# Rotated queries turned by VectorE and carried over a DRAM buffer, their low part made by GpSimd; five queues reordered, scores masked in place

## The chip, the cores and the metric

One core of a Trainium2 chip runs the whole kernel: TensorE (PE), VectorE (DVE), ScalarE (ACT), GpSimd (POOL) and the SyncE queue (SP), which issues most transfers. The metric is the device time of one execution in microseconds (us). All instruction streams are in order; they meet at semaphores written out by hand.

## The reference

Eight sequences of 128 tokens and width 512 go through four residual layers. The change touches only the first, attention over a paged cache:

```
q, k, v = x Wq, x Wk, x Wv          # 32 query heads, 8 key heads, D = 128
q, k = rope(rmsnorm(q)), rope(rmsnorm(k))
keys, values = 16 cached pages of 32 rows (512) + the 128 new ones
scores = q keys^T / sqrt(D), cached keys beyond the length masked
x = x + softmax(scores) values Wo
```

The others are a dense layer with a sign mask, a SwiGLU layer with LoRA, and an adapter product.

## The kernel before, in words

Every fp32 product is made of three passes over a high and a low part (`three_pass`, L65 to L67): ScalarE writes the high part (`hi`, L682), VectorE or GpSimd subtracts it from the source to get the low part (`lo`, L932; GpSimd L541, L546, L550, L555, L561).

Attention loops over 8 groups g (a key head with its 4 query heads) and in each over the 8 sequences b. One (g, b) is called a step here. Groups 1 to 6 are one hardware loop on every engine, group 0 and group 7 are written out. A step works on three sequences at once: it multiplies the probabilities of (g, b) with the values, makes the scores of the next one (g1, b1), and projects the one after that (g2, b2). Each engine has its own `group` function, which lists its work of a step in order. In the order before TensorE does: nine 128x128 transposes of probabilities (heads 0 to 2, chunks 0 to 2), four of the rotated queries of (g1, b1) (`queries`, L1227), three more of probabilities (head 3), the output product of the preceding sequence, the transpose of the new keys (L1221), the query projection of (g2, b2), scores 0 and 1, values 0 and 1, scores 2 and 3, values 2, the key and value projection, values 3 and 4.

Scores leave PSUM by one VectorE instruction that adds the mask, scales, and takes the maximum (`mask_and_max`, L984) into one of two buffers `scores`; ScalarE takes the exponential into `probs` (`exps`, L730), VectorE inverts the sum (`inverse`, L990), GpSimd scales (`normalise`, L565). Chunks 3 and 4 of the probabilities are not transposed by TensorE: VectorE turns their 32x32 squares (`turn_squares`, L1011), SP writes them to the DRAM buffer `turned_rows` (512 KB, L382) and reads them back as four transfers of 128 KB with the squares in their places (L385). ScalarE and VectorE then split them as they do the others (`probs_T`).

Queries: TensorE projects, VectorE multiplies with cosines and sines (`turn_q`, L961 and L963), GpSimd adds (`rotate_q`, L509 and L510), TensorE transposes into bank 4 (L1227), ScalarE copies the high part and VectorE makes the low one (`queries`), and score 0 waits for it on `qT_done`.

In steps b = 1 to 4 of groups 1 to 6 GpSimd also gathers a quarter of the next group's pages into `kv_stage` (`stage_pages`, L497, 1 MB each; in b = 1 and 3 it first computes new page numbers, L492 and L494), and SP stores it in the DRAM buffers `kT_pages` or `v_pages` (L377). Step b = 4 loads the next group's Wq and Wkv (L333, L334), step b = 5 splits them; step b = 0 splits Wo. SP loads keys and values of (g2, b2) in every step (L359, L365). ScalarE splits these values one step later, in (g1, b1)'s place (`cached_values`).

## Time and profile before

| | us |
|---|---|
| median of 3 runs | 1328.85 (1328.2 to 1328.89) |
| profiled execution: its own time / its span | 1327.64 / 1325.9 |
| PE busy | 1302.4 (98%) |
| DVE busy | 1037.4 (78%) |
| ACT / POOL busy | 843.8 / 844.0 (64%) |

The span is what the profile covers, the execution's own time is 1.74 us more. Engines overlap, so the busy times do not add up.

### The profile page before, as it was taken

What the parts mean: (1) busy time and instruction counts of PE and PEld (TensorE: products, weight loads), DVE (VectorE), ACT (ScalarE), POOL (GpSimd) and SP (SyncE); (2) the same over time, 40 slices, a digit from 0 to 9 for tenths busy, and PEclk for the clock granted to TensorE, in tenths of its full rate; (3) what the DMA queues carried; (4) which work ended last, traced back from release to release, by engine and by line L of the source; (5) the groups of instructions that cost most, each with busy time, mean ns of one, the idle gap of its engine ahead of it and who ended that gap; (6) DMA issues with size and microseconds to landing.
All of it is one profiled execution on the core that took longest, in us unless ns stands there. A gap on an engine that the chain in (4) does not pass through costs nothing.

```text
span 1325.9 us, 25249 instructions
## 1 busy us (share of the span) xinstructions
PE 1302.4 (98%) x7316; PEld 1135.4 (86%) x7316; DVE 1037.4 (78%) x2235; ACT 843.8 (64%) x2217; POOL 844.0 (64%) x1116
## 2 busy tenths in 40 slices
PE   9898999999999999999999999999999899999999
PEld 8787888888888888888888888888888688888887
DVE  7977887888787878787888788778888886748546
ACT  7566666766676656666766676666666774635444
POOL 7677777777777767777777786777766832415111
PEclk9999999999999999999999999999999999999999
DMA  5578658745874687468547844884554453454542
GB/s 204 193 212 270 151 143 230 243 127 158 228 215 130 177 238 196 130 183 259 143 127 221 270 110 127 231 274 107 190 132 114 133 171 129 138 177 154 181 140 80
DMA packets 215388, 233.14 MB, mean 176 GB/s; under 512 B 134817, under 2 KB 174369, under 8 KB 204577
## 3 DMA queue, kind: packets, MB, share of 16 engines
q1 hardware_dynamic: 209568, 196.24, 51.0%
q0 software_dynamic: 5760, 36.18, 8.6%
q8 instruction: 29, 0.48, 0.2%
q14 instruction: 31, 0.25, 0.1%
...
## 4 chain that ended last, share of the span: by engine, by line
PE 88%; DVE 8%; POOL 2%; issue 1%; ACT 1%; DMA 1%; SPq 0%; DVEq 0%; POOLq 0%; ACTq 0%
PE ps L65 26%; PE ps L66 25%; PE ps L67 25%; PE ps L1245 5%; DVE at_scores L984 2%; DVE at_pT_lo L932 2%; PE ps L1227 2%; DVE shared L1452 1%; PE ps L2196 1%; PE ps L1287 1%; DMA at_pT_raw<-turned_rows 1%; PE ps L1221 0%; DVE at_turned L1011 0%; POOL at_probs L565 0%; PE ps L2229 0%
## 5 line engine op out<-in xcount | busy, mean ns | idle before, releaser
L730 ACT ACTIVATE at_probs<-at_scores,at_neg_max 128x640 f32<-128x640 f32 x256 | 211.4, 826 | 250.7 <-DVE at_neg_max L984 250.3
L565 POOL TENSOR_SCALAR at_probs<-at_probs,at_row_inv 128x640 f32<-128x640 f32 x256 | 223.1, 876 | 129.7 <-DVE at_row_inv L990 128.5
L984 DVE CUSTOM_DVE_ANT_0 at_scores<-ps,at_mask,at_inv_rms 128x640 f32<-128x640 f32 x256 | 220.3, 879 | 30.8 <-PE ps L67 29.0
L65 PE MATMUL ps<-ds_hi,x_hi 128*128 128x512 f32 (+1 forms) x564 | 198.5, 352 | 0.8 <-DVE x_lo L1502 0.4
L67 PE MATMUL ps<-ds_hi,x_lo 128*128 128x512 f32 (+1 forms) x564 | 192.5, 341 | 0.0
L65 PE MATMUL ps<-at_kT_hi,ds_lo 128*128 128x320 f32 x512 | 159.2, 311 | 9.4 <-DVE at_neg_max L984 6.7
L67 PE MATMUL ps<-at_kT_hi,ds_lo 128*128 128x320 f32 x512 | 158.8, 310 | 0.0
L66 PE MATMUL ps<-at_kT_lo,ds_lo 128*128 128x320 f32 x512 | 158.7, 310 | 0.0
L932 DVE TENSOR_TENSOR at_pT_lo<-ps,at_pT_hi 128x512 fp32r<-128x512 f32 x196 | 133.8, 684 | 7.0
L65 PE MATMUL ps<-at_pT_hi,at_v_hi 128*128 128x512 f32 x320 | 129.6, 405 | 6.6 <-DVE at_pT_lo L932 6.1
L66 PE MATMUL ps<-at_pT_lo,at_v_hi 128*128 128x512 f32 x320 | 126.5, 395 | 0.0
L67 PE MATMUL ps<-at_pT_hi,at_v_lo 128*128 128x512 f32 x320 | 125.3, 391 | 0.0
L65 PEld LDWEIGHTS ps<-ds_hi,x_hi 128*128 128x128 f32 x564 | 106.7, 189 | 19.9 <-DVE x_lo L1502 0.8
L66 PE MATMUL ps<-ds_lo,x_hi 128*128 128x512 f32 x308 | 120.2, 390 | 0.0
L67 PEld LDWEIGHTS ps<-ds_hi,x_lo 128*128 128x128 f32 x564 | 105.9, 188 | 13.1
L509 POOL TENSOR_TENSOR at_q_rot<-ds_bias,a_raw 128x256 f32<-128x256 f32 x64 | 47.5, 741 | 105.7 <-DVE a_raw L963 105.7
L1011 DVE STREAM_TRANSPOSE at_turned<-at_probs 128x256 f32<-128x256 f32 x248 | 97.7, 425 | 18.4 <-POOL at_probs L565 18.4
L65 PEld LDWEIGHTS ps<-at_kT_hi,ds_lo 128*128 128x128 f32 x512 | 96.7, 189 | 17.5 <-DVE at_neg_max L984 8.7
L65 PE MATMUL ps<-at_woT_hi,at_oT_hi 128*128 128x512 f32 x256 | 107.1, 418 | 1.3 <-DVE at_oT_lo L932 1.3
L1245 PE MATMUL ps<-ident,at_probs 128*128 128x128 f32 x784 | 106.4, 272 | 0.0
L682 ACT ACTIVATE at_pT_hi<-ps 128x512 fp32r<-128x512 f32 x196 | 102.5, 600 | 4.3 <-PE ps L67 4.0
L67 PE MATMUL ps<-at_woT_hi,at_oT_lo 128*128 128x512 f32 x256 | 100.7, 394 | 0.0
...
## 6 DMA issues: line engine op xcount, KB each, us to landing
...
kv_raw<-kT_pages SPq DMA_DIRECT2D x60, 256.0 KB, 5.4
...
kv_raw<-v_pages SPq DMA_DIRECT2D x56, 256.0 KB, 4.7
...
```

Of the source, the lines that this page charges most:

```text
L65: pe.matmul(out, l_hi, r_hi, start=first, stop=False)
L66: pe.matmul(out, l_hi, r_lo, start=False, stop=False)
L67: return pe.matmul(out, l_lo, r_hi, start=False, stop=last)
L509: pool.tensor_tensor(q_rot[:, :, 0:HALF], u_q[:, :, 0:HALF], w_q[:, :, HALF:D], ALU.subtract)
L565: pool.tensor_scalar(probs[:, h, :], probs[:, h, :], row_inv[:, h:h + 1], 1.0, ALU.mult, ALU.mult).then_inc(probs_done, 1)
L682: act.activation(out, src, ACT.Copy).then_inc(done, 1)
L730: act.activation(probs[:, h, :], scores[h % 2][:], ACT.Exp, bias=neg_max[:, h:h + 1], scale=-1.0, accum_out=row_sum[:, h:h + 1]).then_inc( ...
L932: dve.tensor_tensor(out, src, hi_part.bitcast(F32), ALU.subtract).then_inc(done, 1)
L984: dve.tensor_tensor_reduce(out=scores[h % 2][:], in0=slot(h), in1=mask[:, b, :], scale=inv_rms[b % 2][:, h:h + 1], scalar=3.0e38, op0=ALU. ...
L1011: dve.transpose(turned[:, :, :, h, :].rearrange("p k c r -> p c k r"), probs[:, h, (KC - MOVED) * P:KEYS].rearrange("p (c k i) -> p c k i" ...
L1227: ins = pe.transpose(bank(Q_BANK)[:, h * S:(h + 1) * S], q_rot[:, h, :], ident[:])
L1245: return pe.transpose(bank(probs_bank(b, c))[:, h * S:(h + 1) * S], probs[:, h, c * P:(c + 1) * P], ident[:])
```

## The change

The rotated queries of all steps but the first two of group 0 no longer go through TensorE. VectorE turns their 32x32 squares in one instruction of 128x512 (`spread_queries`); SP writes them with four transfers into a new DRAM buffer `q_rows` (`store_queries`, 256 KB) and in the next step, right behind the write of `turned_rows`, reads them back with one (`read_queries`, 256 KB). ScalarE makes the high part from there, GpSimd the low part (`queries` of pool).

The orders of all five queues change with it. TensorE projects before it makes the output product, which comes right ahead of score 0, and waits for `y_added` ahead of values 0; score 2 stands between values 0 and 1. VectorE takes its wait for GpSimd's `rotate_q` (in `spread_queries`) ahead of `mask_and_max` 2; the low part of chunk 3 stands ahead of `mask_and_max` 3; heads 0 and 1 share one reciprocal, heads 0 to 2 one turn of squares; the new values' low part moves to the end of the step before, ahead of the last head's squares. GpSimd makes `key_scale` first, then the gather, `cached_keys`, `rotate_k`, `queries`, `cached_values`, the weights' parts, `rotate_q` and the four `normalise`. ScalarE splits cached and new values of (g2, b2) at the end of the step, one step earlier than before, and takes the squares of the queries ahead of the exponentials. One of the two Wq parts that GpSimd made in step b = 6 goes to VectorE in b = 5, the other to GpSimd in b = 5; VectorE's two both stand in b = 5. The masked scores are written into `probs`, and the exponential works there in place. In group 0 GpSimd makes five of the cosine tables in place of four. Four semaphores are merged with others and two added, and single loads of indices are moved in SP's queue of the last group. Of the diff, cut to its core (SP, GpSimd, ScalarE, VectorE, TensorE in this order):

```diff
...
-        scores = [sb(f"scores{j}", [P, KEYS]) for j in range(2)]
...
+        q_turned_rows = sb("q_turned_rows", [P, NQ, G, SQ])
+        qT_raw = sb("qT_raw", [P, NQ, G, SQ])
...
+        def q_by_moves(g, b):
+            return not (isinstance(g, int) and g == 0 and b < 2)
+        def q_moves(g, b, k):
+            return upto(g, b, (NQ + 1) * 16) - 2 * (NQ + 1) * 16 + k * 16
...
+                if not (isinstance(g, int) and (g, b) == (HK - 1, B - 1)) and q_by_moves(*following(g, b)):
+                    read_queries(*following(g, b))
...
+            def store_queries(g, b):
+                wait_apart(sp, q_spread, upto(g, b, 1, 1) - 2, passed)
+                for a in range(NQ):
+                    sp.dma_start(q_rows.rearrange("(k i) (a n) -> a i k n", k=NQ, a=NQ)[a],
+                                 q_turned_rows[a * SQ:(a + 1) * SQ].rearrange("i k h r -> i k (h r)")).then_inc(q_moved, 16)
+            def read_queries(g, b):
+                wait_apart(sp, q_moved, q_moves(g, b, NQ), passed)
+                sp.dma_start(qT_raw[:].rearrange("p a h r -> p (a h r)"), q_rows).then_inc(q_moved, 16)
...
+                    if not (last and b >= B - 2):
+                        store_queries(g2, b2)
...
+            def queries(g, b):
+                wait_apart(pool, qT_hi_done, upto(g, b, 1, 1), passed)
+                l, h = (t[b % 2].rearrange("p (h a r) -> p h a r", h=G, a=NQ) for t in (qT_lo, qT_hi))
+                pool.tensor_tensor(l, qT_raw[:].rearrange("p a h r -> p h a r"), h.bitcast(F32), ALU.subtract).then_inc(qT_done, 1)
...
+                    key_scale(g2, b2)
...
-                    if b == B - 2 and not last:
-                        wq_group(g + 1, 2)
+                    if started and not keys_by_row(g1, b1):
                         cached_keys(g1, b1)
-                        wq_group(g + 1, 3)
-                    key_scale(g2, b2)
-                    if started and not keys_by_row(g1, b1) and b != B - 2:
-                        cached_keys(g1, b1)
+                    rotate_k(g2, b2)
                     if started:
+                        queries(g1, b1)
                         cached_values(g1, b1)
                     if b == B - 3 and not last:
                         qkv_group(g + 1, DC)
...
                     if b == 0:
                         wo_group(g, 0)
                         wo_group(g, 1)
...
                     rotate_q(g2, b2)
-                    normalise(g1, b1, 0)
-                    rotate_k(g2, b2)
-                    for h in range(1, G):
+                    for h in range(G):
                         normalise(g1, b1, h)
...
+                    if b == B - 3 and not last:
+                        wq_group(g + 1, 3)
...
+                if upto(0, b, 1) >= 2 or not (isinstance(g, int) and g == 0):
+                    act.wait_ge(pv_done, upto(g, b, KC) - KC - 1)
...
+                if upto(0, b, 1) >= 2 or not (isinstance(g, int) and g == 0):
+                    act.wait_ge(pv_done, upto(g, b, KC) - KC)
...
-                act.activation(probs[:, h, :], scores[h % 2][:], ACT.Exp, bias=neg_max[:, h:h + 1], scale=-1.0,
+                act.activation(probs[:, h, :], probs[:, h, :], ACT.Exp, bias=neg_max[:, h:h + 1], scale=-1.0,
...
+                if q_by_moves(g, b):
+                    hi(qT_hi[b % 2].rearrange("p (h a r) -> p h a r", h=G, a=NQ), qT_raw[:].rearrange("p a h r -> p h a r"),
+                       q_moved, q_moves(g, b, NQ + 1), qT_hi_done)
...
                         attended(*preceding(g, b))
+                    else:
+                        queries(g1, b1)
+                    probs_T(g, b, 0)
+                    probs_T(g, b, 1)
+                    new_keys(g1, b1)
+                    if started:
                         cached_keys(g1, b1)
-                        new_values(g1, b1)
-                    queries(g1, b1)
+                    probs_T(g, b, 2)
+                    if b == B - 3 and not last:
+                        qkv_group(g + 1, DC)
                     if started:
-                        cached_values(g1, b1)
-                    for c in range(KC - MOVED):
-                        probs_T(g, b, c)
-                    new_keys(g1, b1)
+                        queries(g1, b1)
+                    if b == B - 3 and not last:
+                        qkv_group(g + 1, DC + 1)
...
                             probs_T(g, b, c)
+                    squares(g2, b2)
...
-                        for n in (DC, DC + 1, *range(DC)):
+                        for n in range(DC):
                             qkv_group(g + 1, n)
                     exps(g1, b1, 0)
                     exps(g1, b1, 1)
...
                             probs_T(g, b, c)
                     exps(g1, b1, 2)
                     exps(g1, b1, 3)
-                    squares(g2, b2)
                     if not (last and b == B - 3):
                         key_squares(*following(g2, b2))
+                    cached_values(g2, b2)
+                    new_values(g2, b2)
...
-                dve.tensor_tensor_reduce(out=scores[h % 2][:], in0=slot(h), in1=mask[:, b, :],
+                dve.tensor_tensor_reduce(out=probs[:, h, :], in0=slot(h), in1=mask[:, b, :],
...
+            def two_inverses(g, b):
+                dve.wait_ge(exp_done, upto(g, b, G, 2))
+                dve.reciprocal(row_inv[:, 0:2], row_sum[:, 0:2]).then_inc(inv_done, 2)
...
+            def turn_first_heads(g, b, n):
+                dve.wait_ge(probs_done, upto(g, b, G, n))
+                dve.transpose(turned[:, :, :, 0:n, :].rearrange("p k c h r -> p h c k r"),
+                              probs[:, 0:n, (KC - MOVED) * P:KEYS].rearrange("p h (c k i) -> p h c k i", c=MOVED, k=NQ)).then_inc(turned_done, n)
+            def spread_queries(g, b):
+                dve.wait_ge(q_rot_done, upto(g, b, 1, 1))
+                dve.transpose(q_turned_rows[:].rearrange("p k h r -> p h k r"),
+                              q_rot[:].rearrange("p h (k i) -> p h k i", k=NQ)).then_inc(q_spread, 1)
...
                         attended(*preceding(g, b))
+                    else:
+                        queries(g1, b1)
+                    probs_T(g, b, 0)
                     if b == 1:
                         wo_group(g, 3)
-                    if b == B - 2 and not last:
-                        qkv_group(g + 1, 1)
-                    queries(g1, b1)
+                    probs_T(g, b, 1)
                     if started and keys_by_row(g1, b1):
                         cached_keys(g1, b1)
+                    new_keys(g1, b1)
...
+                        probs_T(g, b, 2)
...
                     if started:
-                        new_values(g1, b1)
-                    probs_T(g, b, 0)
...
+                        turn_k(g2, b2)
+                    turn_q(g2, b2, 0)
+                    turn_q(g2, b2, 1)
                     if started:
-                        add_y(*preceding(g, b), last and b > 0)
-                    probs_T(g, b, 1)
-                    new_keys(g1, b1)
-                    probs_T(g, b, 2)
...
-                        turn_q(g2, b2, 0)
-                        turn_q(g2, b2, 1)
+                        probs_T(g, b, 2)
...
                             probs_T(g, b, c)
...
+                        turn_k(g2, b2)
                     if started:
-                        turn_q(g2, b2, 0)
-                        turn_q(g2, b2, 1)
+                        add_y(*preceding(g, b), last and b > 0)
                     mask_and_max(g1, b1, 0)
                     mask_and_max(g1, b1, 1)
-                    turn_k(g2, b2)
+                    spread_queries(g2, b2)
...
                     if b == 0:
                         wo_group(g, 2)
...
-                    inverse(g1, b1, 0)
                     if b == B - 3 and not last:
                         qkv_group(g + 1, 0)
                     mask_and_max(g1, b1, 2)
-                    inverse(g1, b1, 1)
-                    mask_and_max(g1, b1, 3)
+                    two_inverses(g1, b1)
                     if by_moves(g, b):
                         probs_T(g, b, 3)
...
+                    if b == B - 3 and not last:
+                        qkv_group(g + 1, 1)
+                    mask_and_max(g1, b1, 3)
                     inverse(g1, b1, 2)
                     if by_moves(g, b):
                         probs_T(g, b, 4)
...
+                    if b == B - 3 and not last:
+                        qkv_group(g + 1, 2)
                     inverse(g1, b1, 3)
-                    if by_moves(g1, b1):
-                        for h in range(G):
-                            turn_squares(g1, b1, h)
+                    turn_first_heads(g1, b1, G - 1)
...
+                    new_values(g2, b2)
+                    turn_squares(g1, b1, G - 1)
...
-                    pe.wait_ge(qT_done, upto(g, b, 1))
+                    if by_row(g) and b == 2:
+                        pe.wait_ge(qT_done, 2)
+                    else:
+                        pe.wait_ge(q_squared, upto(g, b, 1))
...
-                    queries(g1, b1)
...
+                        queries(g1, b1)
                     probs_T_rest(g, b)
-                    if started:
-                        output(*preceding(g, b))
                     new_keys(g1, b1)
...
                             probs_T(g, b, c)
                     project_q(g2, b2, range(DC))
+                    if started:
+                        output(*preceding(g, b))
...
                         times_v(g, b, 0)
                         times_v(g, b, 1)
...
                     pe.wait_ge(pT_done, upto(g, b, KC, KC - MOVED if by_moves(g, b) else KC))
                     score(g1, b1, 1)
                     if by_moves(g, b):
+                        pe.wait_ge(*((dense.x1_ready, b) if last and b else (y_added, upto(g, b, 1))))
                         times_v(g, b, 0)
+                    score(g1, b1, 2)
+                    if by_moves(g, b):
                         times_v(g, b, 1)
-                    score(g1, b1, 2)
                     score(g1, b1, 3)
...
```

## Rows read from the trace of the kernel before

**Rows 1.** The page's busy time of each engine, and the chain that ended last.

```profile
PE 1302.4 (98%) x7316; PEld 1135.4 (86%) x7316; DVE 1037.4 (78%) x2235; ACT 843.8 (64%) x2217; POOL 844.0 (64%) x1116
...
PE 88%; DVE 8%; POOL 2%; issue 1%; ACT 1%; DMA 1%; SPq 0%; DVEq 0%; POOLq 0%; ACTq 0%
```

**Rows 2.** By stretch, steps b = 0, 1, 4, 5 of group 1: PE, PEld, DVE, ACT, POOL busy, clock, DMA.

```profile
172.00:188.30 16.30, 16.21 (x97) 14.20 (x95) 13.50 (x32) 12.26 (x34) 12.35 (x17) 1.00 0.38 98
188.30:204.20 15.90, 15.90 (x95) 14.04 (x94) 13.11 (x32) 9.79 (x30) 11.71 (x18) 1.00 0.83 232
...
235.90:251.70 15.80, 15.80 (x94) 13.99 (x93) 12.48 (x31) 10.08 (x30) 11.00 (x16) 1.00 0.97 295
251.70:267.50 15.80, 15.80 (x95) 14.03 (x94) 13.07 (x32) 13.17 (x36) 12.66 (x17) 1.00 0.48 141
```

**Rows 3.** The chain of waits from 616 us (start, length).

```profile
616.62 0.98 PE ps L1245 x9
617.61 0.44 PE ps L1227 x4
618.04 0.33 PE ps L1245 x3
```

**Rows 4.** Transfers, stretches 602.4:604.1 and 636.9:640: packets, MB, share of 16 engines.

```profile
q1 hardware_dynamic: 144, 0.52, 76.4%
...
q1 hardware_dynamic: 528, 0.49, 54.0%
```

**Rows 5.** GpSimd's groups of instructions, 160 to 940 us.

```profile
L565 POOL TENSOR_SCALAR at_probs<-at_probs,at_row_inv 128x640 f32<-128x640 f32 x196 | 170.0, 873 | 97.2 <-DVE at_row_inv L990 97.0
L561 POOL TENSOR_TENSOR at_v_lo<-kv_raw,at_v_hi 128x512 fp32r<-128x512 f32 x50 | 64.4, 1289 | 0.0
...
L509 POOL TENSOR_TENSOR at_q_rot<-ds_bias,a_raw 128x256 f32<-128x256 f32 x49 | 36.1, 738 | 80.2 <-DVE a_raw L963 80.2
```

**Rows 6.** VectorE's timeline in a step b = 5.

```profile
643.30 0.67 DVE L932 TENSOR_TENSOR ds_lo<-staging,ds_hi 128x512 fp32r<-128x512 f32 x1
644.07 0.88 DVE L984 CUSTOM_DVE_ANT_0 at_scores<-ps,at_mask,at_inv_rms 128x640 f32<-128x640 f32 x1
...
645.75 0.82 DVE L932 TENSOR_TENSOR at_pT_lo<-at_pT_raw,at_pT_hi 128x512 fp32r<-128x512 f32 x1
...
647.24 1.15 DVE L1011 STREAM_TRANSPOSE at_turned<-at_probs 128x256 f32<-128x256 f32 x3
```

**Rows 7.** ScalarE's timeline, 603 to 606 us.

```profile
603.28 1.56 ACT L682 ACTIVATE at_pT_hi<-ps 128x512 fp32r<-128x512 f32 x3
605.49 0.28 ACT L682 ACTIVATE at_kT_hi<-ps 128x128 fp32r<-128x128 f32 x1 [0.64 <-PE ps L1221]
```

**Rows 8.** SP's timeline, steps b = 3 and 4.

```profile
601.79 0.33 SPq L382 DMA_DIRECT2D turned_rows<-at_turned  x1
604.48 1.75 SPq L385 DMA_DIRECT2D at_pT_raw<-turned_rows  x4
...
624.99 5.55 SPq L365 DMA_DIRECT2D kv_raw<-v_pages  x1
```

**Rows 9.** GpSimd's timeline: a page number and gather (b = 3), the Wkv parts (b = 5).

```profile
602.48 0.25 POOL L492 TENSOR_SCALAR at_page_row<-at_page_row 128x1 f32<-128x1 f32 x1
...
603.98 1.10 POOL L497 DMA_INDIRECT shared<-in_kT_cache,at_page_idx  x1 [0.89 <-POOL at_page_idx L494]
605.11 0.20 POOL L516 TENSOR_TENSOR at_inv_rms<-at_sumsq,at_d_eps 128x1 f32<-128x1 f32 x1
...
638.14 2.57 POOL L546 TENSOR_TENSOR ds_hi<-at_wkv_raw,ds_hi 128x512 fp32r<-128x512 f32 x2 [0.68 <-ACT ds_hi L682]
```

**Rows 10.** Transfers by issue in b = 4, then b = 5; the last number is us to landing.

```profile
kv_raw<-v_pages SPq DMA_DIRECT2D x1, 256.0 KB, 8.2
...
kv_raw<-v_pages SPq DMA_DIRECT2D x1, 256.0 KB, 4.1
```

**Rows 11.** By stretch, columns as in Rows 2: step b = 3 of group 0.

```profile
85.60:104.30 18.70, 16.57 (x94) 13.90 (x93) 12.96 (x32) 10.18 (x31) 13.38 (x19) 1.00 0.81 211
```

**Rows 12.** By stretch, columns as in Rows 2: a step of group 7.

```profile
983.70:1000.00 16.30, 16.02 (x95) 14.05 (x93) 14.14 (x33) 10.02 (x30) 9.98 (x15) 1.00 0.43 99
```

129 lines of the change are left out of this document (64 added, 65 removed).

## The prediction

> **What bounds the kernel now.** I read the page's first and fourth parts first: TensorE is busy 98% of the span and makes 88% of the chain that ended last [rows 1]. Then the busy time by stretch, step by step: in groups 1 to 6 a step takes 15.8 us and TensorE is busy in all of it, whether the transfer engines are at 0.48 or at 0.97 of their time; only b = 0 takes 16.3 [rows 2]. So in 48 steps every TensorE instruction counts in full, and the other engines have about 3 us of cover each. The chain of waits shows where the removed instructions lie. What the change does to the cover must be read from the orders of the queues.
>
> **What is taken off.** Four transposes, 0.44 us, stand in the chain [rows 3]. 62 steps lose them (64 less the first two): 27.3 us, 0.44 in each, which makes a step of 15.4 us if all else stays hidden. No other TensorE work is added.
>
> **What is added.** On the transfer engines: the write of `turned_rows` moved 0.52 MB in 76.4% of 1.7 us, 1.3 us, and the reads of 1 KB packets 0.49 MB in 54% of 3.1 us, 1.7 us [rows 4]. 256 KB therefore cost 0.65 to 0.85 us; `q_rows` is written and read in each step, and its writes go in packets of 512 B, so 1.7 us a step, 0.11 of a step. On GpSimd: `queries`, 128x512 of two inputs, as L561, 1.29 us [rows 5]. On VectorE: three turns of 128x256 take 1.15 us, so 128x512 takes 0.8, against 0.67 for the low part that leaves [rows 6]. VectorE's sum is unchanged; its order is not.
>
> The Trainium skill ("VectorE: DVE Perf Modes", Rules for kernel authors) says that a 128x128 transpose belongs on TensorE where PSUM will do. By it the 0.44 us on TensorE are the cheap form; the rows say cheap for the other engines only, since TensorE is the one that has no room.
>
> **A plain step, walked.** t counts from the first of the nine transposes. 0.98 + 0.33 [rows 3] end at 1.3; new keys, projection and output (24 matmuls of 0.23 us) end at 7.0, where score 0 is due; the last two value products start at 14.1 and 14.8, and t = 15.4 is the next step. ScalarE gets head 3 at about 1.7, takes two chunks at 0.52, new keys 0.28, cached keys 0.6 [rows 7]: 3.7. GpSimd then makes cached keys 1.25, `rotate_k` 0.6, `queries` 1.25 [rows 5]: 6.8. Score 0 waits for that: 0.2 us of margin. The read of `q_rows` starts behind the turned write, which is issued at about 1.2 and lands 2.7 later [rows 8]; with 0.8 for its own data it lands at 4.7, ScalarE is done at 5.3, GpSimd is free at 5.5. So b = 7 gains its 0.44 in full. GpSimd then makes cached values (8.1) and `rotate_q`, two of 0.74 [rows 5], 9.6; VectorE turns the queries behind `mask_and_max` 1 by 10.4, ahead of score 2: hidden too.
>
> **b = 5 and b = 0.** GpSimd has two weight parts ahead of `rotate_q`, 2.57 us [rows 9]. In b = 5: 8.1 + 2.6 = 10.7, `rotate_q` 12.1, the turn of queries 12.9. VectorE waits in it, and all the rest of its list is queued behind: a Wq part 0.6 (13.5), mask 2 0.8 (14.3), chunk 3 0.8 (15.1), a Wq part 0.6 (15.7), mask 3 0.8 (16.5), chunk 4 0.65 (17.2) [rows 6]. Values 4 are due at 14.8: 2.4 us late, and the normalised heads after it too. Before, only GpSimd's own scaling waited for `rotate_q`. In b = 0 one part less stands there, and none between chunk 3 and mask 3: 16.6 against 14.8, 1.8 us. These two need no assumption on transfers; below, they are 1.2 and 2.0.
>
> **b = 1 to 4.** The gather is issued ahead of `cached_keys`. In b = 1 and 3 it costs GpSimd 2.6 us with its page number (602.48 to 605.11), in b = 2 and 4 1.1 [rows 9]. Head 3's scaling ends at about 0, the two scales add 2.15, 2.6 make 4.8, and 1.25 + 0.6 + 1.25 end at 7.9: score 0 is 0.9 late. A late head 3 adds to it; 0.6 to 1.9, I take 1.0. In b = 2 and 4 GpSimd is in time, but the gather's 1 MB starts while the read of `q_rows` is under way. Alone it lands at 4.7; if it shares the engines to the gather's end it lands up to 1.6 us too late. I take half, 0.8.
>
> The Trainium skill ("DMA: Bandwidth & Descriptors", Queues, rings and completion order) has each transfer engine take turns between queues packet by packet. By that the read would end with the gather, 1.6 us late in both steps, and the sum would be 10 us higher; no row here shows this read beside a gather.
>
> **The values, one step early.** ScalarE's `cached_values` now stands at the end of the step in which its load is issued. In b = 5 that load lands in 4.1 us, in b = 4, behind Wq and Wkv, 8.2 us after 624.99, at 633.2 [rows 8, 10]. The values' last product of that step would end at 616.62 + 15.4 = 632.0 [rows 3]. New values, the attended rows and head 3's squares stand behind it in ScalarE's and VectorE's queues, and TensorE's key transpose waits for the new values' low part. With the engines at 0.97 [rows 2] and 1.7 us more to move, the load comes later still: 1.5 to 3 us, of which some is covered by the late chunk 4 of the next step. I take 0.8 more in b = 5 (3.2 in all) and 0.5 left over in b = 6.
>
> **The sum.** Per group: 1.8 + 1.0 + 0.8 + 1.0 + 0.8 + 3.2 + 0.5 + 0 = 9.1 us of new waits against 8 x 0.44 = 3.5: +5.6, and 6 groups give +33. In group 0 steps take 18.7 us, with GpSimd busy 13.4 of them and transfers at 0.81 [rows 11]: it is bound by the chain through both, which gets 1.3 us of GpSimd and 1.7 of transfers longer. Over five such steps I take +5, between 0 and +10, the 0.44 counted in. In group 7 VectorE is busy 14.1 of 16.3 us [rows 12]; its sum stays, and chunk 4 comes to stand behind a piece of the dense layer's weights: -1 to +3 with the 0.44 counted in, I take 0. 1327.64 + 38 = 1365.6; the profiled execution stood 1.2 us under the median, so 1367 against a median of 1328.85.
>
> Bounds: with the lower ends (1.2, 0.6, 0, 0.6, 0, 2.0, 0, 0 = 4.4 a group) +0.9 a group, 5 in all, and -1 outside: 1333. With the upper ends (1.8, 1.9, 1.6, 1.9, 1.6, 4.5, 0.7, 0 = 14.0) +10.5 a group, 63, and +13 outside: 1405.
>
> **The rivals.**
> A, this forecast, new waits outweigh the transposes: 1333 to 1385.
> B, the other side: GpSimd and VectorE catch up, so the waits are not lost. The place is `rotate_q` ahead of the turn of queries in b = 0 and b = 5; if VectorE's late list costs TensorE under 3.5 us a group in all, the kernel is faster. For it: before, TensorE had no wait in b = 5 with GpSimd at 12.7 busy of 15.8 [rows 2]. Against: the walk gives 4.2 in these two steps alone. With nothing late it is 1328.85 - 27.3 = 1301.5, with half the lower ends 1315.
> C, transfers become the bound. b = 4 at 0.97 plus 0.11 no longer fits in its step, and what is left pushes the turned write, chunks 3 and 4, and the values of the next. For it: 0.83 in b = 1 becomes 0.94. Against: b = 0 and 5 stay under 0.6 with it. 1385 to 1405.
> D, gains and waits cancel: within 0.2% of before, which is about what a measurement of this kernel can tell from no change.
>
> A 0.55, B 0.20, C 0.20, D 0.05. So slower 0.75, same 0.05, faster 0.20. The range takes A, D, most of C and the near part of B: 1315 to 1398; A's own is 1333 to 1385.
>
> **What would show it.** L1227 down to 8 transposes. In the chain of waits of b = 0 and 5, VectorE at L984 and L932, released by GpSimd at L509; a wait of the turn of queries for GpSimd of 2 us there and none in b = 7. Score 0 late by GpSimd's `queries` in b = 1 and 3. ScalarE waiting for `v_pages` in b = 4. Steps of 15.4 us for b = 7, about 17 for b = 0, 18 for b = 5. The prediction is wrong if TensorE's idle time stays under 3.5 us a group: then GpSimd's list ran earlier than walked, or `rotate_q` was not late.

## The result and the profile after

The changed kernel takes 1426.85 us in the median of 4 runs (1424.84 to 1429.76), the kernel before 1328.53 (4 runs): a ratio of 1.0742, 95% interval 1.0723 to 1.0761. It is slower, as forecast, but by 98 us where 38 were forecast, and outside the range of 1315 to 1398. The profiled execution took 1429.76 us for a span of 1427.9, 102.0 above the span before.

The page, busy time and then the chain that ended last, answers to [rows 1]:

```profile
PE 1305.6 (91%) x7068; PEld 1108.7 (78%) x7068; DVE 1038.7 (73%) x2054; ACT 856.8 (60%) x2217; POOL 938.4 (66%) x1173
...
PE 46%; DMA 16%; DVE 11%; POOL 11%; issue 9%; SPq 3%; ACT 3%; POOLq 0%; DVEq 0%; ACTq 0%
```

TensorE was 88% of the chain and is 46%; transfers, VectorE and GpSimd share the rest. The stretch of groups 1 to 6, first before and then after, shows where it went (length, then PE, PEld, DVE, ACT, POOL busy, clock, DMA share, GB/s):

```profile
172.00:935.50 763.50, 762.94 (x4420) 673.66 (x4418) 616.97 (x1465) 510.02 (x1453) 554.97 (x757) 1.00 0.65 186
```

```profile
184.50:1031.10 846.60, 765.67 (x4225) 651.57 (x4224) 621.63 (x1327) 520.70 (x1452) 626.49 (x799) 0.99 0.72 197
```

In these 48 steps TensorE had 0.6 us of idle time before and has 80.9 after. It has 192 transposes fewer, 21 us by [rows 3], and is still busy 2.7 us longer: what is left runs longer. The three parts of the 102.0: 12.5 us in group 0 (group 1 starts at 184.5 against 172.0), 83.1 in groups 1 to 6, 6.4 behind. The steps of group 1, b = 0, 1, 4 and 5, answer to [rows 2]:

```profile
184.48:202.56 18.08, 16.34 (x92) 13.80 (x91) 13.25 (x29) 12.67 (x34) 13.82 (x18) 1.00 0.47 117
202.56:219.96 17.40, 15.68 (x90) 13.48 (x89) 12.84 (x29) 10.26 (x30) 13.37 (x19) 1.00 0.88 240
255.46:274.51 19.05, 15.91 (x90) 13.46 (x89) 12.85 (x28) 10.28 (x30) 13.75 (x19) 0.99 0.90 274
274.51:294.38 19.87, 17.89 (x83) 15.00 (x82) 14.25 (x31) 12.97 (x35) 14.07 (x14) 0.84 0.49 134
```

Here and below a step's length is the time from one issue of the turned write to the next, mean over groups 2 to 6:

```
b              0     1     2     3     4     5     6     7    sum
before       16.4  15.9  15.8  15.8  15.8  15.8  15.8  15.8  127.3
after        19.9  17.8  15.9  17.1  18.4  19.9  15.6  16.0  140.8
forecast     17.2  16.4  16.2  16.4  16.2  18.6  15.9  15.4  132.3
```

The waits of the changed kernel (engine, what it does, who releases it: us in all, times, longest):

```profile
ACT ds_lo L716 <- DMA at_qT_raw<-q_rows: 102.4, 57, 3.2
PEld ps L65 <- issue: 78.9, 59, 3.7
...
DVE at_q_turned_rows L1072 <- POOL at_q_rot L540: 32.7, 16, 3.0
...
PE ps L65 <- POOL ds_lo L590: 22.8, 11, 3.3
...
ACT at_v_hi L716 <- DMA kv_raw<-v_pages: 14.5, 6, 3.4
ACT at_oT_hi L716 <- issue: 13.5, 5, 3.0
PE ps L1284 <- DVE at_v_lo L1024: 12.8, 7, 2.9
```

The waits that the forecast named are there: ScalarE waits for the value pages six times, VectorE for `rotate_q` 16 times, TensorE for GpSimd's low part. The lengths are not: b = 7, 0 and 5 take 16.0, 19.9 and 19.9 us where 15.4, about 17 and 18 were forecast. Two rows were not in it. ScalarE waits for the queries' read in nearly every step, and five times 2.7 us for nothing visible ("issue").

### The profile page after: what moved, and what is told of

Read it like the earlier page. It is cut to its first block, busy times and chain, and to the rows that moved or that the text cites. A ratio compares the mean times of both kernels' runs of the same rounds, so it can differ in the third digit from the quotient of the medians.

```text
span 1427.9 us, 25340 instructions
## 1 busy us (share of the span) xinstructions
PE 1305.6 (91%) x7068; PEld 1108.7 (78%) x7068; DVE 1038.7 (73%) x2054; ACT 856.8 (60%) x2217; POOL 938.4 (66%) x1173
## 4 chain that ended last, share of the span: by engine, by line
PE 46%; DMA 16%; DVE 11%; POOL 11%; issue 9%; SPq 3%; ACT 3%; POOLq 0%; DVEq 0%; ACTq 0%
PE ps L65 14%; PE ps L66 13%; PE ps L67 13%; DMA at_pT_raw<-turned_rows 6%; DMA kv_raw<-v_pages 4%; DMA turned_rows<-at_turned 3%; DVE at_probs L1031 3%; POOL at_probs L600 3%; PE ps L1308 2%; DVE at_pT_lo L979 2%; DMA at_qT_raw<-q_rows 2%; SPq L401 2%; POOL at_woT_lo L580 1%; DVE at_turned L1066 1%; POOL ds_hi L576 1%
## 5 line engine op out<-in xcount | busy, mean ns | idle before, releaser
L600 POOL TENSOR_SCALAR at_probs<-at_probs,at_row_inv 128x640 f32<-128x640 f32 x256 | 250.9, 990 | 176.8 <-DVE at_row_inv L1041 150.6
L768 ACT ACTIVATE at_probs<-at_probs,at_neg_max 128x640 f32<-128x640 f32 x256 | 211.8, 828 | 223.7 <-DVE at_neg_max L1031 223.7
L1031 DVE CUSTOM_DVE_ANT_0 at_probs<-ps,at_mask,at_inv_rms 128x640 f32<-128x640 f32 x256 | 224.2, 881 | 96.6 <-PE ps L67 93.6
L979 DVE TENSOR_TENSOR at_pT_lo<-ps,at_pT_hi 128x512 fp32r<-128x512 f32 x196 | 128.8, 681 | 4.2 <-ACT at_pT_hi L716 4.2
L66 PE MATMUL ps<-at_pT_lo,at_v_hi 128*128 128x512 f32 x320 | 127.3, 398 | 0.0
L716 ACT ACTIVATE at_pT_hi<-ps 128x512 fp32r<-128x512 f32 x196 | 111.1, 602 | 26.4 <-PE ps L1308 22.1
L979 DVE TENSOR_TENSOR at_pT_lo<-at_pT_raw,at_pT_hi 128x512 fp32r<-128x512 f32 x124 | 106.4, 858 | 21.2 <-ACT at_pT_hi L716 21.1
L67 PEld LDWEIGHTS ps<-ds_hi,x_lo 128*128 128x128 f32 x564 | 106.7, 189 | 13.5
L585 POOL TENSOR_TENSOR at_kT_lo<-kv_raw,at_kT_hi 128x512 fp32r<-128x512 f32 x60 | 77.1, 1286 | 45.1 <-ACT at_kT_hi L716 44.3
L65 PEld LDWEIGHTS ps<-at_pT_hi,at_v_hi 128*128 128x128 f32 x320 | 60.6, 189 | 57.6 <-DVE at_pT_lo L979 55.4
L65 PE MATMUL ps<-at_woT_hi,at_oT_hi 128*128 128x512 f32 x256 | 100.5, 393 | 1.5 <-DVE at_oT_lo L979 1.4
L1308 PE MATMUL ps<-ident,at_probs 128*128 128x128 f32 x784 | 100.6, 277 | 1.1 <-POOL at_probs L600 0.9
```

The source lines that it names most:

```text
L65: pe.matmul(out, l_hi, r_hi, start=first, stop=False)
L66: pe.matmul(out, l_hi, r_lo, start=False, stop=False)
L67: return pe.matmul(out, l_lo, r_hi, start=False, stop=last)
L585: pool.tensor_tensor(in_pages(kT_lo[:, 0:L]), pages_keys(k_raw[b % 2]), in_pages(kT_hi[:, 0:L]).bitcast(F32), ALU.subtract).then_inc(kc_do ...
L600: pool.tensor_scalar(probs[:, h, :], probs[:, h, :], row_inv[:, h:h + 1], 1.0, ALU.mult, ALU.mult).then_inc(probs_done, 1)
L716: act.activation(out, src, ACT.Copy).then_inc(done, 1)
```

## The experiments

A ratio is against the kernel before.

**e1, e2, e3, e4: single waits, and what the transposes were worth.** In e1 `spread_queries` moves behind the fourth mask:

```diff
                     mask_and_max(g1, b1, 1)
-                    spread_queries(g2, b2)
...
                     mask_and_max(g1, b1, 3)
+                    spread_queries(g2, b2)
```

> The changed kernel with one move: VectorE's turn of the rotated queries (and with it its wait for GpSimd's rotate_q) stands behind the fourth score's mask instead of behind the second's. Theory 1 (VectorE's wait in b=0 and b=5 is on the path): the changed kernel waits 16 times for rotate_q, 32.7 us in all, 2.0 us each, with masks 2 and 3 queued behind; with the move these waits vanish and the time falls by 16 to 32 us, to 1395 to 1411. Theory 2 (the trip of the queries over DRAM is the path): the turn starts some 3 us later in six of eight steps, the read lands as much later, ScalarE's wait for it (102.4 us in all, 57 times) grows, and the time stays or rises, to 1425 to 1460. Theory 3 (GpSimd's own order, rotate_q behind the parts of wo and wkv, sets these steps whatever waits on VectorE): within 5 us of 1427.

It took 1498.69 us (1.1271, 1.1251 to 1.1291), 72 us more than the change: theory 2, the trip over DRAM is on the path, and by more than was thought. ScalarE's wait for the read rose:

```profile
ACT ds_lo L716 <- DMA at_qT_raw<-q_rows: 173.8, 62, 5.0
```

Not all of the 72 us is waiting: TensorE's busy time rose from 1305.6 to 1339.0 us at a mean granted clock of 0.962 against 0.993.

e2 issues the read ahead of SyncE's wait for the turned probabilities:

```diff
                     if by_moves(g, b):
+                        if q_by_moves(*following(g, b)):
+                            wait_apart(sp, qT_done, upto(g, b, 1, 1), passed)
+                            read_queries(*following(g, b))
                         move_turned(g, b)
```

> The changed kernel with one move on the DMA issuing queue: the read of the turned queries is issued ahead of SyncE's wait for the turned probabilities (once the raw buffer's last reader is through), not behind it and behind the write. Theory 1 (ScalarE's wait for that read, 1.8 us in nearly every step, holds squares and the exps behind it and so the path): the wait falls below 0.5 us and the time falls by 60 us or more, to under 1370. Theory 2 (the wait is idle time that ScalarE has over, since the exps behind it wait for scores anyway): the wait vanishes and the time falls by under 10 us, 1417 to 1427. Theory 3 (the DMA engines are the bound in the tail of the step): the read now delays other transfers, above all the gather's, and the time is within 5 us or slower.

It took 1406.64 (1.0576, 1.0557 to 1.0595), 20 us less than the change, between theories 1 and 2. The wait fell from 102.4 us to this:

```profile
ACT ds_lo L717 <- DMA at_qT_raw<-q_rows: 11.5, 11, 4.6
```

Of 91 us of ScalarE's waiting 20 were on the path. The step b = 7 fell from 16.0 to 15.3 us: the plain step of the forecast, 15.4, is there once the read is in time. b = 5 fell by 1.3 us too, and b = 0 rose from 19.9 to 20.7.

e3 puts ScalarE's and VectorE's halves of the values back into the following step:

```diff
-                    cached_values(g2, b2)
-                    new_values(g2, b2)
...
                     if started:
+                        new_values(g1, b1)
                         attended(*preceding(g, b))
...
                         queries(g1, b1)
+                        cached_values(g1, b1)
```

> The changed kernel with ScalarE's and VectorE's halves of the values put back into the following step, where the kernel before had them (new values ahead of the attended values, cached values behind the queries). Theory 1 (in b=4 ScalarE waits 2.1 us for the value pages and with it everything behind, 14.5 us over six groups; TensorE waits 12.8 us more, seven times, for the new values behind): both waits vanish, b=4 is shorter by 2 to 3 us, and the time falls by 15 to 25 us, to 1402 to 1412. Theory 2 (the halves cost the same wherever they stand, and in the following step they lie ahead of the probabilities' eviction, on the path): the six steps without a wait grow by about 1 us each and the time rises by 20 to 50 us.

It took 1424.8 (1.0713, 1.0694 to 1.0732), 2 us less. b = 4 fell from 18.4 to 16.6 us, as theory 1 said, but b = 0 and b = 5 rose from 19.9 to 21.5 and 21.1, as theory 2 did. The value pages' wait was real, and taking it away by this move was worth nothing.

e4 leaves three of four query transposes out of the kernel before, from (0, 2) on, so heads 1 to 3 score with old queries:

```diff
-                for h in range(G):
+                for h in range(1 if upto(0, b, 1) >= 2 or not (isinstance(g, int) and g == 0) else G):
                     ins = pe.transpose(bank(Q_BANK)[:, h * S:(h + 1) * S], q_rot[:, h, :], ident[:])
```

> The kernel before with one of the four query transposes on TensorE in each step from the second group's start on (heads 1 to 3 of the bank then hold old queries): what the three transposes' TensorE time, 0.33 us by the row of the chain, is worth by itself, with nothing else moved. Theory 1 (TensorE's stream sets every step, the prediction's term of 0.44 us for four): the time falls by 0.33 x 62 = 20 us, to 1308. Theory 2 (the steps are set by the evictions on VectorE and ScalarE, which stay): it falls by under 7 us, 1322 to 1329.

It took 1329.52 (0.9996, 0.9986 to 1.0006): theory 1 fell. Three quarters of the saving that the forecast credited at 0.44 us a step are worth nothing in the old order. The chain of waits of e4 over a step shows why (lines of TensorE left out between 460.51 and 471.32):

```profile
459.87 0.60 DVE at_oT_lo L932
460.47 0.04 issue
460.51 0.50 PE ps L65
...
471.58 0.80 DVE at_scores L984
472.38 0.01 DVE at_neg_max L984
472.39 0.74 DVE at_pT_lo L932
...
474.44 0.81 POOL at_probs L565
475.26 0.02 issue
475.28 0.45 DVE at_turned L1011
475.73 0.59 DVE at_oT_lo L932
```

From the attended values' low part (459.87) through TensorE's output product, projection and scores to the fourth mask, its normalisation, its turn and the next attended low part (475.73) it is 15.86 us, and the transposes are not in it. The kernel before had two loops of one length, TensorE's own and this one. TensorE at 98% busy showed only the first.

**e5, e8, e9: trip or reordering?** e5 is the changed order with the queries turned on TensorE again:

```diff
                     probs_T_part(g, b)
-                    if not started:
-                        queries(g1, b1)
+                    queries(g1, b1)
                     probs_T_rest(g, b)
...
-                    spread_queries(g2, b2)
...
-                        store_queries(g2, b2)
```

> The changed kernel with the rotated queries turned on TensorE again (transposes ahead of the last head's probabilities, high part by ScalarE and low part by VectorE out of the bank, right behind the attended values, as the kernel before had them); no VectorE spread, no store, no read, no low part on GpSimd. All other reorderings of the change stay. Theory 1 (the trip of the queries over DRAM costs the time): 1330 to 1350, within 2% of the kernel before. Theory 2 (the reordered queues cost it, GpSimd's four normalisations in one burst and the output behind the projection above all): 1395 to 1430. Halves: near 1375.

It took 1416.27 (1.0644, 1.0625 to 1.0663). That looked like theory 2, the reordering costs it all. But the kernel has a wait that neither parent has:

```profile
PE ps L65 <- DVE ds_lo L949: 71.6, 61, 2.9
```

The projection waits for the queries' low part in the bank that it writes. In the kernel before, the output product stood between them. So e5 doesn't price the reordering by itself.

e8 is the kernel before with the scores in place and the five DMAs of the queries added, unused; e9 has the scores in place alone:

```diff
+                    if not (last and b >= B - 2):
+                        store_queries(g2, b2)          # e8: out of q_rot, read into a tile that nobody uses
...
-                dve.tensor_tensor_reduce(out=scores[h % 2][:], in0=slot(h), in1=mask[:, b, :],
+                dve.tensor_tensor_reduce(out=probs[:, h, :], in0=slot(h), in1=mask[:, b, :],
```

> The kernel before with the scores masked in place and, added, the store of the rotated queries (four DMAs) and the read (one) at the same places of SyncE's queue as in the change; the queries still go over TensorE, what is read is used by nobody. It prices the traffic and the issuing alone. Theory 1 (the traffic and the waits in SyncE's queue are hidden, only the dependence of the scores on the trip costs): within 5 us of the kernel before, 1325 to 1335. Theory 2 (the DMA engines or SyncE's queue are near their bound in the tail of the step, so the read of the turned probabilities and the loads behind land later): 1350 to 1400.

> The kernel before with one edit: the scores are masked into the probabilities' tile and the exp works in place there; the two score tiles are gone. No engine gets more work. Both theories of the change take it as free: 1326 to 1331. Should the mask of a head have to wait for that head's probabilities of the step before, it would cost 0.5 us or more a step, over 1360.

e9 took 1330.01 (1.0002, 0.9993 to 1.0012): free. e8 took 1341.37 (1.0089, 1.0072 to 1.0105): traffic and issuing cost 12 us, and 6.9 of them lie in group 0 (group 1 starts at 178.9 against 172.0). In groups 2 to 6 the eight steps add up to 127.7 us against 127.3, with b = 4 longer by 1.1 and b = 5 shorter by 0.9. (In e8 GpSimd's `rotate_q` also waits for an earlier store, so the 12 us are an upper price for traffic and issuing.) Nobody waits for the read here. So the load on the transfer engines isn't the cause by itself; what waiting for the landing costs, e8 doesn't tell.

**e7, e6: moves together, and the wait for `rotate_q` alone.** e7 joins e2 and e3 and moves `rotate_q` ahead of GpSimd's weight parts; e6 does the last alone:

```diff
                         cached_values(g1, b1)
+                    rotate_q(g2, b2)
                     if b == B - 3 and not last:
                         qkv_group(g + 1, DC)
...
-                    rotate_q(g2, b2)
```

> The changed kernel with three moves together: the read issued ahead of SyncE's wait for the turned probabilities (alone it gave 1406.6), ScalarE's and VectorE's halves of the values back in the following step (alone 1424.8), and GpSimd's rotate_q in b=0 and b=5 ahead of the parts of wo and wkv. If the waits that each removes are separate: 20 us, 2 us and, for 16 waits of 2 us, 15 to 30 us, so 1375 to 1390. If the steps with these waits are set by something behind them all (the turned probabilities' trip, or GpSimd's burst): 1400 to 1407, the read alone.

> The changed kernel with GpSimd's rotate_q ahead of the parts of wo (b=0) and of wkv (b=5), where VectorE waits 2.0 us for it. The prediction charged 3.2 us a group to b=5 and 1.8 to b=0 for this. If it was right, the time falls by up to 30 us, to 1397; if the weights' parts only come later and hold up what waits for them, or another wait lies right behind, it falls by under 8 us.

e6 took 1406.85 (1.0587, 1.057 to 1.0605), 20 us less: b = 0 from 19.9 to 18.2 us and b = 5 from 19.9 to 18.4. The forecast's place was right. e7 took 1395.92 (1.0504, 1.0479 to 1.0529), 31 us less where the three parts give 42.

**e10: ScalarE's jump back.** The five waits for "issue" lie at the start of groups 2 to 6. ScalarE's timeline there:

```profile
606.34 0.28 ACT L757 ACTIVATE at_v_hi<-ps 128x128 fp32r<-128x128 f32 x1
609.22 0.60 ACT L716 ACTIVATE at_oT_hi<-ps 128x512 fp32r<-128x512 f32 x1 [2.60 <-issue]
```

```diff
-            with act.Fori(1, HK - 1) as g:
+            for g in range(1, HK - 1):
                 group(g, False)
```

> The changed kernel with ScalarE's loop over groups 1 to 6 written out as straight code; the other engines keep their loops, and every engine has the same operations in the same order. In the changed kernel ScalarE waits 2.4 to 3.0 us for nothing that the profile shows ahead of the attended values in b=0, in just the five groups that begin with a jump back (13.5 us in all), and the steps of b=0 last 19.9 us where the kernel before had 16.3. Theory 1 (the jump back makes ScalarE wait for its instructions, and the change has put an operation that waits for TensorE last in the loop, so that no queued work covers the jump): the five waits vanish and the time falls by 10 to 15 us, to 1412 to 1417. Theory 2 (the wait is for something else at the group's start, say for what the weights' parts of the new group need): no change, within 4 us of 1427.

It took 1415.98 (1.0651, 1.0618 to 1.0683), 11 us less; the five waits are gone and b = 0 fell to 18.1 us. The page's row of the queue that brings instructions (packets, MB, share) tells what they were; first before, then after, then e10:

```profile
q14 instruction: 31, 0.25, 0.1%
```

```profile
q14 instruction: 56, 0.46, 0.1%
```

```profile
q14 instruction: 41, 0.34, 0.1%
```

The changed kernel moves 25 packets of instructions more, and the waits stand right behind a jump back. The kernel before has no such wait: there ScalarE stood idle for 0.25 us ahead of the same operation, for TensorE:

```profile
552.77 0.60 ACT L682 ACTIVATE at_oT_hi<-ps 128x512 fp32r<-128x512 f32 x1 [0.25 <-PE ps L67]
```

The Trainium skill ("Runtime: NRT & Kernel Launch", Instruction fetch mechanics) says that a taken branch whose target isn't among the two pages that an engine holds must fetch it by DMA before it goes on; the traces agree (waits of 2.5 to 3.0 us and 56 packets with the jump, no wait and 41 packets without). No run measured the size at which ScalarE's loop stops fitting.

**e11, e12, e13: single orders put back.** e11 is e5 with the output product ahead of the projection; e12 and e13 are the change with one VectorE order undone:

```diff
                     probs_T_rest(g, b)
+                    if started:
+                        output(*preceding(g, b))       # e11
...
+                    inverse(g1, b1, 0)                 # e12
                     mask_and_max(g1, b1, 2)
-                    two_inverses(g1, b1)
+                    inverse(g1, b1, 1)
...
                     mask_and_max(g1, b1, 3)
+                    if by_moves(g, b):                 # e13, ahead of the mask in the change
+                        probs_T(g, b, 3)
```

> The kernel with the queries turned on TensorE and the changed orders (it took 1416.3) with one more thing put back: TensorE's output product of the attended values stands ahead of the projection of the queries, as in the kernel before. There the projection waited 1.15 us in nearly every step (71.6 us in all, 61 times) for VectorE's low part of the queries, in the bank that it writes to. Theory 1 (that wait is all that the plain steps of that kernel lose): plain steps fall from 16.9 to about 15.9 and the time to 1350 to 1365; what is left over the kernel before is the price of the other reorderings. Theory 2 (output's own inputs, the attended values' low part, are as late as the queries' low part): 1400 to 1416.

> The changed kernel with the inverses of heads 0 and 1 made apart again, head 0's ahead of the third mask and head 1's behind it, so that GpSimd can start its four normalisations earlier. Theory 1 (in many steps the burst of four, 3.81 us, ends 1 us behind the last inverse and so delays the turn and with it the whole trip of the probabilities): plain steps get shorter by 0.5 to 1 us and the time falls by 20 to 50 us. Theory 2 (the last normalisation waits for the last inverse anyway): within 6 us, and the added instruction on VectorE, 0.15 us a step, may cost up to 9.

> The changed kernel with VectorE's low part of the first moved chunk of the probabilities behind the fourth mask again, as in the kernel before; it is ahead of it in the change, so that a late landing of the turned probabilities holds up the fourth mask, its exp, its normalisation and the next turn, the loop from trip to trip. Theory 1 (that loop sets b=1, b=3 and b=4, where ScalarE is seen to wait for the landing): each of these shorter by 0.5 to 1 us, 10 to 18 us in all, 1409 to 1417. Theory 2 (the landing also holds ScalarE's exps, so the loop goes on through them): within 5 us of 1427.

e12 took 1419.8 (1.0674, 1.065 to 1.0698), 7 us less, just over theory 2's bound; the plain steps b = 6 and 7 stayed at 15.6 and 16.1. e13 took 1435.37 (1.0794, 1.0771 to 1.0818), 8 us more: both theories fell. e11 took 1455.5 (1.0954, 1.0923 to 1.0984), 39 more than e5. Its waits:

```profile
ACT at_kT_hi L693 <- PE ps L1244: 138.5, 61, 4.1
...
PEld ps L65 <- DVE at_pT_lo L949: 106.1, 85, 2.0
```

The output product put the new keys' transpose later, and the change has ScalarE wait for those keys ahead of the cached keys and the third chunk. One order put back into a set that was made for another only makes a new wait.

**e15, e14: the trip in the old order, and the best of the new.** e15 is the kernel before with the trip and nothing else of the reordering (and the scores in place). e14 is the change with e3, e6, e10 and e12, and e2's read in all steps but b = 0.

```diff
                     inverse(g1, b1, 0)
+                    spread_queries(g2, b2)             # e15, VectorE
...
                     for c in range(KC - MOVED):
                         probs_T(g, b, c)
+                    if started:
+                        queries(g1, b1)                # e15, ScalarE, out of qT_raw
```

> The kernel before with the trip of the queries alone, and every queue else in its old order: VectorE spreads the rotated queries ahead of the third mask, SyncE stores and reads them as in the change, ScalarE takes the high part behind the first probabilities' evictions, GpSimd the low part ahead of its low part of the cached values, TensorE turns none. Scores masked in place. Theory 1 (the trip costs what its transfers cost, 12 us, and its late landing some 20 more at most; the rest of the 98 us is the reordering): 1335 to 1365. Theory 2 (the trip is the cost, and the reordering is what it takes to bear it): 1400 or more.

> The changed kernel with what helped, together: the read ahead of the wait for the turned probabilities in all steps but b=0, the halves of the values in the following step, rotate_q ahead of the parts of wo and wkv, the inverses of heads 0 and 1 apart, ScalarE's loop written out. Three of these together took 1395.9; the inverses gave 7 us and the loop 11 us alone. If these are separate costs: 1375 to 1382. If one hides another: 1385 to 1396. Either way it stays over the kernel before, unless the steps of b=0 to b=5 fall to 16 us, which no part so far did.

e15 took 1428.46 (1.0739, 1.0721 to 1.0757): theory 1 fell clearly. The trip put into the old order costs just what the whole change costs. Its plain steps b = 2 and b = 7 are 15.8 us, as before: without the transposes, and nothing gained. Its b = 0 and b = 5 take 22.4 and 20.0 us. ScalarE in b = 0, and its wait in all:

```profile
601.40 0.23 ACT L752 ACTIVATION_READ_ACCUMULATOR at_square<-ps 128x1 f32 x1
606.00 0.60 ACT L718 ACTIVATE at_oT_hi<-ps 128x512 fp32r<-128x512 f32 x1 [4.37 <-issue]
```

```profile
ACT ds_lo L718 <- DMA at_qT_raw<-q_rows: 109.3, 57, 5.1
```

The jump back costs it 22.6 us in five waits of ScalarE, the longest 5.1. Like e5, e15 has a wait of its own making: its high part of the queries stands in ScalarE's queue ahead of the new keys' (in the change, behind them), so what ScalarE waits for the read holds up the keys too. So its 99 us are the price of the trip at this place of the queue. No run has it at another place in the old order. e14 took 1369.89 (1.0303, 1.0286 to 1.032), 57 us less than the change and better than its expectation; it is the best version of the change that ran, and slower than the kernel before. Its plain steps are 15.0 and 15.3 us; b = 1 to 5 take 16.3 to 18.2.

**e16, e17: ScalarE's squares.** e16 is the kernel before with one call moved; e17 moves it in the changed kernel:

```diff
+                    squares(g2, b2)                    # e16, ahead of the weights of wo and wq
                     if b == 0:
                         for n in range(WO_GROUPS):
                             wo_group(g, n)
...
                     exps(g1, b1, 3)
-                    squares(g2, b2)
```

> The kernel before with ScalarE's squares of the next queries ahead of the exps, where the change has them, instead of behind them. In the kernel before, four squares that wait for nothing stand behind the last exp and ahead of the key's square and the jump back, and ScalarE starts the new group's attended values 0.25 us after TensorE releases them. Theory 1 (these squares cover the jump back): five steps of b=0 get up to 2.5 us longer, up to 12 us in all, 1333 to 1342, with a wait for nothing visible ahead of the attended values. Theory 2 (the jump back costs only where a TensorE wait stands last, the key's square, which stays where it is, or something else covers it): within 3 us of 1329.

> The changed kernel with ScalarE's squares of the next queries behind the weights' evictions (four of wo in b=0, the rest of the q weights in b=5), still ahead of the exps. Theory 1 (the squares wait for VectorE's turned queries, and the weights' evictions, 2.2 us and more, which used to fill that wait, now stand behind it and delay the exps: e16 showed 3.0 us in b=0 and 3.5 in b=5 for it in the kernel before): b=0 and b=5 shorter by 1.5 to 3 us each, the time lower by 18 to 36 us, 1391 to 1409. Theory 2 (in the changed kernel these two steps are held by rotate_q and the weights' parts on GpSimd, 20 us in e6, and the squares are second to that): lower by under 8 us.

e16 took 1380.53 (1.0377, 1.036 to 1.0394), 51 us more than before, by a cause that neither theory had. No wait for "issue" appeared. b = 0 and b = 5 rose to 19.3 and 19.4 us and b = 6 to 16.8, the others by 0.3 at most. ScalarE in b = 0:

```profile
591.04 0.28 ACT L725 ACTIVATE at_square<-ps 128x128 bf16<-128x128 f32 x1 [3.78 <-DVE a_raw L963]
...
592.05 2.21 ACT L682 ACTIVATE at_woT_hi<-staging 128x512 fp32r<-128x512 f32 x4
594.14 0.84 ACT L730 ACTIVATE at_probs<-at_scores,at_neg_max 128x640 f32<-128x640 f32 x1
```

The four weights' evictions, 2.2 us, stood ahead of the exps before and the squares behind them. Now the squares wait 3.78 us for VectorE's turned queries, and the evictions, which could have run in that time, come behind that wait and hold up the exps. In e17, where the squares go behind them again but in the changed kernel, nothing came back: 1430.41 (1.0766, 1.0746 to 1.0785). Theory 2 held there: other waits stand in these two steps.

**e18: the weights' load.** It is e14 with the squares of e17 and, in b = 4, the next group's weights loaded behind the store of the queries:

```diff
-                    if not last and b == 4:
-                        ...
-                        load_qkv(g + 1)
...
                         store_queries(g2, b2)
+                    if not last and b == 4:
+                        ...
+                        load_qkv(g + 1)
```

> The version of the changed kernel that took 1369.9 with two more moves: the squares behind the weights' evictions, and in b=4 SyncE's load of the next group's weights behind the store of the queries instead of ahead of the key and value pages (the pages' issue took 6.1 to 6.4 us behind it, and the store of the queries waited for that). If both work as thought: b=4 falls from 18.2 to about 16.5, b=5 by 1 to 2 us more, b=0 is at 16.6 already, so 1345 to 1360. If the weights' load then collides with the turned probabilities' trip of b=5: b=5 grows by what b=4 gives, 1365 to 1372. Under 1329 is expected by neither: b=1 and b=3 stay at 16.8 by the landing of the turned probabilities.

It took 1387.84 (1.045, 1.0433 to 1.0468), 18 more than e14. b = 4 fell from 18.2 to 16.1 us (e17, the squares alone, had left it at 18.3), so for e14 the cause is right: SyncE needs 6.23 us there to issue the value pages behind the weights, the store of the queries stands behind it, and the turned write, for which VectorE is ready at 660.7, is issued at 663.1:

```profile
660.32 0.40 DVE L1065 STREAM_TRANSPOSE at_turned<-at_probs 128x256 f32<-128x256 f32 x1
```

```profile
663.12 1.07 SPq L396 DMA_DIRECT2D turned_rows<-at_turned  x1
```

In the changed kernel SyncE needs as long, but there the turned write is issued at 696.88, 0.1 us behind VectorE's turn. What holds b = 4 there is the value pages' landing, for which ScalarE waits 2.05 us until 695.31; SyncE's queue came to the fore with that wait gone and the read put ahead of the turned write (e7 and e14 take 18.2 us in b = 4, e3 alone 16.6). SyncE of the changed kernel in b = 4, with [rows 8]:

```profile
684.06 0.36 SPq L347 DMA_DIRECT2D staging<-in_L_cond_Wq  x1
684.60 0.80 SPq L348 DMA_DIRECT2D at_wkv_raw<-in_L_cond_Wkv  x1
685.81 0.41 SPq L373 DMA_DIRECT2D kv_raw<-kT_pages  x1
686.31 6.36 SPq L379 DMA_DIRECT2D kv_raw<-v_pages  x1
692.79 2.15 SPq L408 DMA_DIRECT2D q_rows<-at_q_turned_rows  x4
```

But in e18 the turned write stands behind the weights, its reads are issued 9.1 us after it instead of 2.7, and b = 5 takes 21.5 us:

```profile
665.02 0.32 SPq L396 DMA_DIRECT2D turned_rows<-at_turned  x1
674.15 1.74 SPq L401 DMA_DIRECT2D at_pT_raw<-turned_rows  x4
```

## Why the prediction was right in sign and wrong in size

**The step that failed** is "The sum": 9.1 us of new waits a group. By the table of steps, against the plain step of 15.4, they were 4.5 + 2.4 + 0.5 + 1.7 + 3.0 + 4.5 + 0.2 + 0.6 = 17.4 (0.5 of the 4.5 in b = 0 was there before, in a step of 16.4). Groups 1 to 6 were sized +33 and gave +83.1, which is 50 of the 64 us that are missing in the profiled execution (102 against 38); group 0 was sized +5 and gave +12.5, what lies behind group 6 was sized 0 and gave +6.4. b = 0, 1 and 4 lie above their own upper ends of 1.8, 1.9 and 1.6. The mechanism, new waits that outweigh the transposes, is what the traces show, and every place that was named has its wait.

TensorE's idle time in groups 2 to 6, 13.4 us a group, tells which waits were mis-sized. Ahead of the values, where the walk of b = 0 and b = 5 put 1.8 and 2.4 us for chunks 3 and 4, TensorE waits 1.7 and 2.2: sized right. Ahead of score 0 it waits 1.4, 1.7, 0.3, 1.4, 0.3, 1.2, 0.1 and 0.5 us in b = 0 to 7, 6.9 in all, where the sum had 3.6 (b = 1 to 4) and nothing in b = 0, 5 and 7. In group 4 score 0 starts 0.1 us behind the end of GpSimd's low part of the queries in each of the seven steps with such a wait, whatever releaser the rows name. So the path that the forecast sized too small is the one through ScalarE's high and GpSimd's low part of the queries to score 0. The step lengths have 4 us a group more than this idle time has. Part of it lies at the edges of the waits: in b = 5 of group 3 matmuls of 128x512 start 0.23 us apart, but the last ahead of a wait takes its full 0.39, and the first behind it holds the next for 0.34. That makes an estimated 0.27 us a wait. By terms:

- *Plain step, 15.4 us (b = 7).* The walk said that the read lands at 4.7, ScalarE is done at 5.3 and score 0 is due at 7.0. In group 4 the transposes start at 731.85 and:

```profile
737.23 0.63 ACT L716 ACTIVATE ds_lo<-at_qT_raw 128x512 fp32r<-128x512 f32 x1 [1.83 <-DMA at_qT_raw<-q_rows]
```

```profile
738.04 1.27 POOL L590 TENSOR_TENSOR ds_lo<-at_qT_raw,ds_lo 128x512 fp32r<-128x512 f32 x1 [0.98 <-ACT ds_lo L716]
```

```profile
739.41 0.38 PE L65 MATMUL ps<-at_kT_hi,ds_lo 128*128 128x320 f32 x1 [0.49 <-issue]
```

  The landing is at 5.4, GpSimd ends at 7.5, and score 0 starts at 7.6 where it was due at 7.1. The walk was right but for 0.7 us of landing, and its margin was 0.2. e2, which takes the landing away, has 15.3; e3 and e10, where ScalarE starts on the read 0.5 us sooner in this step, have 15.3 and 15.5.
- *The gain, 0.44 us a step.* Right in the new order (15.0 to 15.3 us in e2 and e14), nothing in the old (e4, and e15's 15.8). The forecast took it from TensorE's busy share alone. It missed the second loop. In the new order the output product stands behind the projection, which would take the projection out of that loop; that this is what makes room for the gain was not tested by itself.
- *b = 5, 3.2 us; b = 0, 1.8 us.* Both measured 4.5. VectorE's wait for `rotate_q` came as walked, 2.04 us against "a wait of 2 us", and e6 gives 1.5 and 1.7 us for it. In b = 0 the jump back adds 1.8 (e10), of which no row before told: it is the wait ahead of score 0 there, of which e10 leaves 0.3 us at most in groups 2 to 4. In b = 5 that wait has another cause, the read of the queries. In group 4 it lands 4.1 us after its issue, where b = 7 has 3.6, and e2, which issues it sooner, leaves 0.2 us of the wait or nothing:

```profile
701.51 0.63 ACT L716 ACTIVATE ds_lo<-at_qT_raw 128x512 fp32r<-128x512 f32 x1 [2.25 <-DMA at_qT_raw<-q_rows]
```

```profile
702.32 1.27 POOL L590 TENSOR_TENSOR ds_lo<-at_qT_raw,ds_lo 128x512 fp32r<-128x512 f32 x1 [1.94 <-ACT ds_lo L716]
```

  VectorE in b = 5, against [rows 6]:

```profile
708.80 0.71 DVE L1072 STREAM_TRANSPOSE at_q_turned_rows<-at_q_rot 128x512 f32<-128x512 f32 x1 [2.04 <-POOL at_q_rot L540]
...
710.00 0.88 DVE L1031 CUSTOM_DVE_ANT_0 at_probs<-ps,at_mask,at_inv_rms 128x640 f32<-128x640 f32 x1
```

- *b = 4, 0.8 us.* Measured 3.0. The forecast saw the value pages come late and priced them in b = 5 and 6. The wait is in b = 4 itself: VectorE's last turn of squares stands behind the new values' low part, and with it the turned write. e3 takes 1.8 us off it. Left out too was SyncE's queue: the forecast had the 5.55 us of issuing in [rows 8], and did not put the store of the queries and the turned write behind it. In the changed kernel that queue is just in time; in e14 it costs 2.1 us (e18).
- *b = 2, 0.8 us.* Measured 0.5. The forecast took from the rule of the Trainium skill ("DMA: Bandwidth & Descriptors", Queues, rings and completion order) that the read would end with the gather, 1.6 us late. It doesn't: in group 4 the read lands 3.1 us after its issue, sooner than the 3.6 of b = 7 without a gather, and the gather, issued 1 us later, takes 6.2. That settles the 1.6; it is no test of the rule that the engines take turns.
- *b = 1 and 3, 1.0 each.* Measured 2.4 and 1.7, with TensorE waiting for GpSimd's low part of the queries as said (22.8 us in 11 waits). e2 takes 0.8 off b = 1 and nothing off b = 3. In group 4's b = 1 head 3's scaling ends 0.6 us behind the first transpose, where the walk had 0 (before, it was 0.4 already), and page number and gather take 3.0 us for 2.6; GpSimd's low part ends at 8.7 for 7.9, in b = 3 at 8.3. What else lengthens these two steps stays open.

**The rivals.** C, transfers become the bound, would have given 1385 to 1405; e8 shows 12 us for traffic and issuing where nobody waits for the read, so the load on the engines isn't the distance to the forecast. When the read lands is another matter: e1 and e2 show it on the path. B, the other side, and D fell with the result.

**Open.** How the 98 us divide into trip and reordering isn't shown: the trip in the old order costs 99 us (e15) and the change 98 with both. e5 and e11 tried to price the reordering alone, e15 the trip alone, and each brought a wait of its own. Shown is where all of them lose: b = 0 and b = 5, where ScalarE has 2.2 us and more of weights to evict, take 17.7 to 22.4 us in e5, e11, e15, e16 and the change. Of the kernels with the new orders only e14, and e18 that is built on it, had b = 0 under 17 us. e7, with three of its five moves, had 20.9 there; ScalarE's loop written out, the inverses apart and the read left late in b = 0 make the difference, and how they share it wasn't told apart. e14 is still 41 us over the kernel before, and no run tells where all of these lie.
